# A two-layer cross-attention block on one core: the second layer attends over plain memory rows, the first loads are rearranged, and every engine follows a new sequence of steps

## The reference

```python
x = rms_norm(hidden, ln_in_w)
mixed = where(vm, x @ v_qkv, x @ l_qkv)          # two experts, chosen by token types
q, k, v = split(mixed); rotary on q, k           # 16 heads of 16
hidden += where(vm, ctx @ v_dense, ctx @ l_dense) # ctx: causal self-attention within a sequence
hidden += cross_attention(rms_norm(hidden), encoder)   # 16 heads of 8
m = rms_norm(hidden)                             # SwiGLU, inner width 688, two experts
hidden += where(vm, mlp(m, v_gate, v_up, v_down), mlp(m, l_gate, l_up, l_down))
```

```python
mem = M @ W_mem.T
mc = softmax(h @ mem.T / 16) @ mem
g = sigmoid(concat(h, mc) @ W_gate.T + b_gate)
out = rms_norm(h + g * mc) * norm_w
```

## Time and profile before

| | us |
|---|---|
| median of 3 runs | 482.73 |
| lowest and highest run | 481.61, 486.07 |
| span of the profiled execution | 474.8 |
| PE busy | 427.1 (90%) |
| DVE busy | 355.7 (75%) |
| ACT busy | 252.7 (53%) |
| POOL busy | 134.3 (28%) |

### The profile page before, as it was taken

How to read it: one execution, slowest core, us unless ns; L and a number is a source line. 1 busy time by engine, 2 the same in 40 slices (tenths; PEclk the granted TensorE clock), 3 DMA queues, 4 the chain that set the end, 5 groups by cost and what they waited for, 6 DMA issues and landing times.

```text
span 474.8 us, 10858 instructions
## 1 busy us (share of the span) xinstructions
PE 427.1 (90%) x3844; PEld 333.2 (70%) x3844; DVE 355.7 (75%) x810; ACT 252.7 (53%) x706; POOL 134.3 (28%) x246
## 2 busy tenths in 40 slices
PE   1769989899699999999999999999998999799992
PEld 1648767776468679678677777867866688487882
DVE  4888898877887898798699699699784466056575
ACT  3354458667644555556565475564462444466652
POOL 3475213232242032124114204203022100436323
PEclk9998999999989999999999999999998999999997
DMA  7813243864421112102102202111004100213111
GB/s 231 296 58 113 65 150 120 259 220 161 138 68 57 35 31 94 46 24 85 62 12 79 80 1 79 59 33 30 19 23 133 46 23 11 77 46 101 55 43 58
DMA packets 27314, 39.44 MB, mean 83 GB/s; under 512 B 3968, under 2 KB 21376, under 8 KB 27264
## 3 DMA queue, kind: packets, MB, share of 16 engines
q1 hardware_dynamic: 24128, 28.24, 18.4%
q0 software_dynamic: 3136, 10.52, 6.8%
HBM read 25.12 MB, written 13.63 MB: 82 GB/s over the span
## 4 chain that ended last, share of the span: by engine, by line
PE 66%; DVE 18%; ACT 6%; DMA 4%; issue 4%; POOL 1%; SPq 1%; POOLq 0%; ACTq 0%; DVEq 0%
PE b_ps L1653 7%; PE xyz L1540 6%; PE xyz L1499 6%; PE xyz L1526 4%; PE b_ps L1407 4%; DVE E L1144 4%; PE b_ps L1656 3%; PE b_ps L1409 3%; DVE mx L1142 3%; PE b_ps L1408 3%; PE xyz L1738 2%; PE xyz L1407 2%; PE xyz L1409 2%; PE xyz L1408 2%; PE b_ps L1667 2%
## 5 line engine op out<-in xcount | busy, mean ns | idle before, releaser
L1142 DVE TENSOR_REDUCE mx<-xyz 128x8 f32<-128x512 f32 x64 | 43.7, 683 | 5.8 <-PE xyz L1499 5.2
L1499 PE MATMUL xyz<-kT,qT 32*64 32x128 f32 (+1 forms) x768 | 44.1, 328 | 2.3 <-DVE kT L265 0.7
L1144 DVE TENSOR_TENSOR E<-xyz,mx 128x512 f32<-128x512 f32 x64 | 44.3, 691 | 2.2
L1526 PE MATMUL xyz<-cst,E 128*128 128x128 f32 x256 | 36.3, 279 | 3.6 <-ACT E L827 2.7
L259 POOL TENSOR_TENSOR qk<-E 128x256 f32<-128x256 f32 x16 | 14.2, 885 | 87.5 <-DVE E L1124 87.5
L1653 PE MATMUL b_ps<-w_gu_hi,ms_hi 128*128 (+2 forms) x90 | 37.9, 421 | 1.0 <-ACT ms_hi L851 0.6
L863 ACT ACTIVATE th<-b_ps,mrh 128x256 f32<-128x256 f32 (+1 forms) x45 | 20.2, 449 | 33.2 <-PE b_ps L1656 33.2
L1540 PEld LDWEIGHTS xyz<-vb,kT 128*64 128x64 f32 x1024 | 32.4, 138 | 6.9 <-issue 4.8
L1540 PE MATMUL xyz<-vb,kT 128*64 128x18 f32 (+1 forms) x1024 | 34.8, 219 | 2.3 <-DVE kT L1194 1.8
L1526 PEld LDWEIGHTS xyz<-cst,E 128*128 128x128 f32 x256 | 29.2, 142 | 10.3 <-ACT E L827 6.6
L1499 PEld LDWEIGHTS xyz<-kT,qT 32*64 32x64 f32 x768 | 20.7, 134 | 20.8 <-issue 9.0
(11 more groups left out here) (322 smaller groups left out, 1221.5 us busy)
## 6 DMA issues: line engine op xcount, KB each, us to landing
qkv_rows<-qrow SPq DMA_DIRECT2D x13, 384.0 KB, 2.6
...
```

The costliest lines, as they stand in the source:

```text
L1142: dve.tensor_reduce(mx[:, t, heads], s, AX.X, ALU.max).then_inc(max_ready, 1)
L1144: dve.tensor_tensor(E[t][:, b * 512:(b + 1) * 512].rearrange("p (h k) -> p h k", k=SEQ), s, mx[:, t, heads].unsqueeze(2).to_broadcast([P, ...
L1499: last = pe.matmul(xy[t][q, hp, o:o + w], qT[t][rows, c, q], kT[t][rows, (2 * c + b) * w:(2 * c + b + 1) * w], start=not masked, stop=True ...
L1526: last = pe.transpose(xy[t][:, a // 4, (a % 4) * P:(a % 4 + 1) * P], E[t][:, a * P:(a + 1) * P], ident)
```

## The change

Layer 1: `mem` exists for eight steps only. A step k transposes the plain memory of tiles 2k and 2k+1 (`mem_rows`) and makes the projected keys of tile k (`mem_keys`) in the same bank; ACT copies all with one instruction. So tiles 0 to 7 have their keys projected ahead and skip `hw`; their scores are h times keys, two products. Tiles 8 to 15 keep `hw` and the scores over plain memory. For all tiles a new step `mctx` weighs the plain memory rows, ACT copies the result, and `gate` multiplies it with `w_memT` (512 columns in one product), in place of the two products with projected memory. The wait for a free set moves from `mem` to `h3T`.

Start: the constants come in two transfers (`load_id`, `load_cst`), and all first loads stand in SP's list (W0: load_types:0 load_ln:0 load_id:0 q_in:0 q_in:1 load_cst:0, then load_w:0 to load_w:3, load_xs:2, q_in:2, load_ca:0, load_zero:0, load_w:4, load_w:5, load_xs:3, q_in:3, load_xs:1). A copy of one column is ACT's first instruction. The first products wait for each chunk of a split weight and not for both.

Order: all lists of all stages are new. In the middle stages the same step of both tiles mostly stands side by side, one `qkT` and sometimes a `cdense` cross a stage's border, and in W2 DVE and POOL begin with rope:4 and rope:5. The diff, cut to its core:

```diff
-        mpg = [late_piece(u, H, 3 * H) for u in range(NB)]
+        mcT = [late_piece(u, H, H + P) for u in range(NB)]
+        mem_rows = [late_piece(i // 2, 4 * H + i % 2 * P, 4 * H + (i % 2 + 1) * P) for i in range(N_TILES)]
+        mem_keys = [late_piece(u, 5 * H, 6 * H).rearrange("p (c k) -> p c k", c=HC) for u in range(NB)]
         mw = [late_piece(u, 3 * H, 3 * H + P) for u in range(NB)]
         hwT = mw
         mwT = [late_piece(u, 3 * H + P, 4 * H) for u in range(NB)]
-        z = [late_piece(u, 4 * H, 5 * H) for u in range(NB)]
-        w_gate2 = mpg[1].rearrange("p (c n) -> p c n", c=HC)
+        w_gate2 = late_piece(1, H, 3 * H).rearrange("p (c n) -> p c n", c=HC)
...
             ("W0", dict(
...
                 dve="""
-                    route_t:0 rank:0 wsplit:0 rank2:0 q_T:0 wsplit:1 wsplit:2 wsplit:3 q_T:1 pos:0 q_out:0 rank3:0
-                    q_out:1 q_T:2 q_out:2 table:0 rope:0 q_out:3 rope:1 qkT:0 wsplit:4 q_out:4 qkT:1 score:0 score:1
...
+                    route_t:0 pos:0 q_T:0 wsplit:0 wsplit:1 rank:0 table:0 wsplit:2 wsplit:3 q_out:0 rank2:0 q_T:1 rank3:0
+                    q_out:1 rope:0 q_T:2 q_out:2 q_out:3 rope:1 qkT:0 qkT:1 q_out:4 score:0 score:1 q_out:5 probT:0
...
                 pool="""
-                    q_sq:0 q_sq:1 x_sort:4 x_sort:5 x_sort:6 x_sort:7 rope:0 rope:1 q_sq:2 x_sort:8 x_sort:9 x_sort:10
-                    x_sort:11 x_sort:12 x_sort:13 x_sort:14 x_sort:15 q_sq:3 q_sq:4 q_sq:5 dense:0 q_sq:6 dense:1
-                    q_sq:7 rope:2 q_sq:8 rope:3""",
+                    q_sq:0 q_sq:1 x_sort:4 x_sort:5 x_sort:6 rope:0 x_sort:7 rope:1 q_sq:2 x_sort:8 x_sort:9 x_sort:10
+                    x_sort:11 x_sort:12 x_sort:13 x_sort:14 x_sort:15 q_sq:3 q_sq:4 q_sq:5 q_sq:6 dense:0 dense:1""",
...
             ("W3", dict(
...
                 dve="""
-                    qkT:6 qkT:7 score:6 miT:2 score:7 gu0:2 gu1:2 probT:6 probT:7 gu2:2 hT0:2 pv:6 pv:7 hT1:2 ctxT:6
-                    dense:6 ctxT:7 miT:3 down:2 dense:7 gu0:3 cscore:6 gu1:3 cscore:7 gu2:3 cprobT:6 hT0:3 cprobT:7
-                    hT1:3 cpv:6 rope:8 cpv:7 rope:9 cdense:6 down:3 cdense:7""",
+                    qkT:6 qkT:7 miT:2 down:1 score:6 gu0:2 score:7 gu1:2 gu2:2 probT:6 probT:7 hT0:2 hT1:2 pv:6 pv:7
+                    ctxT:6 ctxT:7 miT:3 down:2 dense:6 dense:7 gu0:3 cscore:6 cscore:7 gu1:3 gu2:3 cprobT:6 cprobT:7 hT0:3
+                    hT1:3 rope:8 cpv:6 cpv:7 rope:9 cdense:6 cdense:7""",
...
                 pe="""
-                    qkT:6 qkT:7 score_a:6 score:6 score_a:7 miT:2 score:7 gu0:2 probT:6 gu1:2 probT:7 gu2:2 hT0:2 pv:6
-                    pv:7 hT1:2 ctxT:6 ctxT:7 miT:3 dense:6 down:2 h1T:6 dense:7 cproj:6 gu0:3 cscore_a:6 h1T:7
-                    cscore:6 cproj:7 gu1:3 cscore_a:7 cscore:7 gu2:3 cprobT:6 hT0:3 cprobT:7 hT1:3 cpv:6 cpv:7 cctxT:6
-                    down:3 cctxT:7 cdense:6 cdense:7""",
+                    miT:2 qkT:7 score_a:6 score_a:7 score:6 gu0:2 score:7 gu1:2 gu2:2 probT:6 probT:7 hT0:2 hT1:2 pv:6
+                    pv:7 miT:3 ctxT:6 ctxT:7 down:2 dense:6 dense:7 h1T:6 gu0:3 h1T:7 cproj:6 cproj:7 cscore_a:6
+                    cscore_a:7 cscore:6 cscore:7 gu1:3 gu2:3 cprobT:6 cprobT:7 hT0:3 hT1:3 cpv:6 cpv:7 down:3 cctxT:6
+                    cctxT:7 qkT:8 cdense:6 cdense:7""",
             ("W7", dict(
                 sp="""
-                    m_in:10 m_in:11 m_out:10 m_out:11""",
+                    m_in:10 m_out:9 load_x:14 load_ca:14 m_in:11 m_in:12 load_cb:0 m_out:10 m_out:11""",
...
                 pool="""
-                    m_sq:10 sort:12 m_sq:11 dense:14 dense:15 sort:13""",
+                    rope:14 rope:15 sort:12 sort:13 dense:14 m_sq:11 dense:15""",
...
             ("MID", dict(
...
                 pe="""
-                    miT:12 gu0:12 gu1:12 gu2:12 hT0:12 mem:0 mem:1 hT1:12 down:12 miT:13 miT:14 gu0:13 gu1:13 gu2:13
-                    gu0:14 miT:15 hT0:13 hT1:13 gu1:14 down:13 hT0:14 gu2:14 gu0:15 gu1:15 hT1:14 down:14 miT:16
-                    gu2:15 hT0:15 gu0:16 hT1:15 gu1:16 gu2:16 down:15 hT0:16 hT1:16 mem:2 down:16 mem:3 mem:4 mem:5
-                    mem:6 mem:7""",
+                    gu0:12 gu1:12 gu2:12 hT0:12 hT1:12 mem:0 down:12 miT:13 miT:14 gu0:13 gu1:13 gu2:13 gu0:14 hT0:13
+                    hT1:13 miT:15 gu1:14 down:13 gu2:14 gu0:15 hT0:14 hT1:14 gu1:15 gu2:15 down:14 miT:16 hT0:15 hT1:15
+                    gu0:16 gu1:16 down:15 gu2:16 hT0:16 hT1:16 down:16 mem:1 mem:2 mem:3 mem:4 mem:5 mem:6 mem:7""",
             ("L1", dict(
...
                 pe="""
-                    h3T:0 hw:0 h3T:1 hw:1 h3T:2 mscore:0 h3T:3 mscore:1 hw:2 hw:3 h3T:4 attnT:0 mscore:2 mscore:3
-                    gate:0 attnT:1 hw:4 h3T:5 h3T:6 h3T:7 mscore:4 attnT:2 gate:1 mem:8 gate:2 attnT:3 hw:5 hw:6
-                    attnT:4 mscore:5 h3T:8 mem:9 mscore:6 hw:7 gate:3 gate:4 hw:8 attnT:5 h3T:9 mem:10 gate:5 h3T:10
-                    mscore:7 attnT:6 mscore:8 hw:9 mem:11 mem:12 hw:10 h3T:11 attnT:7 attnT:8 mscore:9 mscore:10
-                    gate:6 hw:11 attnT:9 mem:13 gate:7 mscore:11 h3T:12 mem:14 h3T:13 gate:8 attnT:10 h3T:14 mem:15
-                    hw:12 hw:13 h3T:15 attnT:11 mscore:12 hw:14 gate:9 mscore:13 mscore:14 hw:15 attnT:12 gate:10
-                    attnT:13 gate:11 attnT:14 mscore:15 gate:12 gate:13 attnT:15 gate:14 gate:15""",
+                    h3T:0 h3T:1 mscore:0 mscore:1 h3T:2 attnT:0 h3T:3 mscore:2 attnT:1 mctx:0 mscore:3 h3T:4 mctx:1 gate:0
+                    h3T:5 gate:1 attnT:2 attnT:3 h3T:6 h3T:7 mscore:4 mscore:5 h3T:8 mscore:6 mctx:2 mscore:7 hw:8 mctx:3
+                    gate:2 attnT:4 attnT:5 gate:3 mctx:4 mctx:5 mscore:8 h3T:9 attnT:6 attnT:7 gate:4 mctx:6 mctx:7 h3T:10
+                    gate:5 h3T:11 gate:6 h3T:12 gate:7 h3T:13 attnT:8 hw:9 h3T:14 hw:10 hw:11 hw:12 hw:13 h3T:15 mscore:9
+                    mscore:10 hw:14 mscore:11 hw:15 mctx:8 mscore:12 mscore:13 attnT:9 gate:8 attnT:10 attnT:11 mctx:9
+                    attnT:12 mscore:14 mctx:10 attnT:13 mscore:15 gate:9 attnT:14 mctx:11 attnT:15 mctx:12 mctx:13 gate:10
+                    mctx:14 mctx:15 gate:11 gate:12 gate:13 gate:14 gate:15""",
-            sp.dma_start(types_t[:, :, :].rearrange("p a i -> p (a i)"), d["types_t"]).then_inc(S["ld_cst"], 16)
-            sp.dma_start(cst[:, :], d["consts"]).then_inc(S["ld_cst"], 16)
-            sp.dma_start(ln[:, :, :].rearrange("p i c -> p (i c)"), d["ln"]).then_inc(S["ld_ln"], 16)
+            def load_types(n, t):
+                sp.dma_start(types_t[:, :, :].rearrange("p a i -> p (a i)"), d["types_t"]).then_inc(S["ld_types"], 16)
+
+            def load_id(n, t):
+                sp.dma_start(ident, d["consts"][:, C_ID:C_ID + P]).then_inc(S["ld_id"], 16)
+
+            def load_cst(n, t):
+                sp.dma_start(cst[:, C_ID + P:C_END], d["consts"][:, C_ID + P:C_END]).then_inc(S["ld_cst"], 16)
+
+            def load_ln(n, t):
+                sp.dma_start(ln[:, :, :].rearrange("p i c -> p (i c)"), d["ln"]).then_inc(S["ld_ln"], 16)
+
...
             def mem(n, t):
-                u, turn = late_set(n, t)
-                act.wait_ge(S["mem_ps"], tl(n, t))
-                act.activation(mpg[u], L[u], ACT.Copy, scale=0.5).then_inc(S["mem_ready"], 1)
+                k = index(n, t)
+                act.wait_ge(S["mem_ps"], k + 1)
+                act.activation(late_piece(k, 4 * H, 6 * H), L[k], ACT.Copy, scale=H ** -0.5).then_inc(S["mem_ready"], 1)
...
-                act.wait_ge(S["hw_ps"], tl(n, t))
+                act.wait_ge(S["hw_ps"], tl(n, t) - NB)
...
+            def mctx(n, t):
+                u, turn = late_set(n, t)
+                act.wait_ge(S["mc_ps"], tl(n, t))
+                act.activation(mcT[u], L[u][:, 0:P], ACT.Copy, scale=0.5 * H ** 0.5).then_inc(S["mc_ready"], 1)
...
+            act.wait_ge(S["blank"], 1)
+            act.activation(ss4[:, 0:1], m_sqr[:, 0:1], ACT.Copy).then_inc(S["table_in"], 1)
+            act.wait_ge(S["table_in"], 1)
...
-                dve.wait_ge(S["ld_cst"], 32)
+                dve.wait_ge(S["ld_id"], 16)
                 dve.tensor_copy(ident_h[:, :], ident)
                 dve.tensor_tensor(ident_q[:, :, :], ident[:, 0:SEQ].unsqueeze(1).to_broadcast([P, 2, SEQ]),
                                   ident[:, SEQ:P].unsqueeze(1).to_broadcast([P, 2, SEQ]), ALU.add)
+                dve.wait_ge(S["ld_cst"], 16)
...
-                if r < 2:
-                    pe.wait_ge(S["wsplit_lo"], HC * (r + 1))
                 for c in range(HC):
+                    if r < 2:
+                        pe.wait_ge(S["wsplit_lo"], HC * r + c + 1)
...
             def mem(n, t):
-                i, (u, turn) = index(n, t), late_set(n, t)
-                if i == 0:
+                k = index(n, t)
+                if k == 0:
                     pe.wait_ge(S["ld_cb"], 16 * 4)
                     pe.wait_ge(S["catt_ready"], N_TILES)
-                if turn:
```

(45 more changed lines are left out.)

270 lines of the change are left out of this document (133 added, 137 removed).

## The result

The changed kernel took 478.06 us (476.57 to 479.4, 9 runs), the kernel before 482.73 (480.49 to 486.07, 9 runs): a ratio of 0.9895 [0.987, 0.992], 4.7 us less, where 13.2 less was forecast. The time lies in my range and the sign is right; the gain is a third of the forecast one. The profiled execution took 476.7 us for a span of 474.5.

The account below looks back on a forecast made before the run. PE was taken as the bound, DVE close behind in the middle and a mixture before W2. Terms -5.2, -1.0, -3.5, -2.0, -1.5 and 0 sum to -13.2 us, from 482.7 to 469.5, range 459 to 480.

Parts of the forecast that it names:

- The last layer, -5.2: Layer 1: less PE work from dropped `mem` and `hw` steps, saving 5.2 us net, bounds -6.5 and -2.
- MID, -1.0 and -3.5: MID: fewer `mem` steps before `down:16` save 1.0 us; expert slot 12's wait and low clock at its start go, 3.5.
- Start -2.0: Kernel start: earlier table load, first product and `x_sort` issues save 2.0 us, bounds 0 and -4.5.
- W0 to W2 -1.5: New order at 126 to 132 us: PE waits less for DVE's splits and ropes, saving 1.5 us, bounds +2 and -4.
- W2 to W6, order. The work is the same ... I book 0.: Middle stages: reordered steps move stalls without net gain, 0 us booked, bounds -1.2 and +1.2 a stage over six stages.
- The sign that I had named: Middle stages: the prediction is wrong if the steady period leaves 37.3 to 39.3 us, or L1 saves less than 3.
- So 7.9 us lie around the span: Whole kernel before: median run 482.73 us against a 474.8 us span, with 7.9 us taken to lie around the span.
- B: Rival, whole kernel: only L1's counted saving of 5.2 us arrives, MID and start gains are given back; 477.5 us, chance 0.14.
- D: Rival, no change: L1's saving is lost to new waits and stages cost 0.8 us each; 479.5, up to 483, chance 0.12.

Follow-up runs that it names:

- z1: The changed kernel, unaltered, on a chip where the kernel before takes 477.19 us: 463.81 us, ratio 0.9721.
- v2: The kernel before, unaltered, run again with a profile on a chip where it takes 482.63 us: 483.87 us, ratio 1.0018.
- v4: The changed kernel, unaltered, on a chip where the kernel before takes 482.63 us: 477.46 us, ratio 0.9908.
- x1: The kernel before with only layer 1 new (lists and code), old start and old lists through MID: 472.13 us against 476.98, ratio 0.9896.
- v1: The changed kernel with old lists in W3 to W6, miT:10 and m_sq:10 moved at the join to W7: 474.46 us against the kernel before's 482.63, ratio 0.9838.
- y2: The changed kernel with old lists in W3 to W6, run again on a chip where the kernel before takes 477.02 us: 465.97 us, ratio 0.9769.

## Why the forecast came out as it did

Both kinds of chip have a pair of profiles. The start of the second h2 sum of a group, of the last y and the end of the last `fin`, in us (the first column is the trace of before that I worked from):

| | before | z1 | difference | v2 (before) | v4 (after) | difference |
|---|---|---|---|---|---|---|
| group 0 | 78.4 | 77.3 | -1.1 | 81.5 | 83.7 | +2.2 |
| group 2 | 171.2 | 165.7 | -5.5 | 177.3 | 173.0 | -4.3 |
| group 6 | 324.5 | 318.8 | -5.7 | 330.7 | 330.4 | -0.3 |
| group 7 | 362.8 | 357.0 | -5.9 | 369.0 | 369.4 | +0.4 |
| last y | 405.3 | 395.5 | -9.8 | 410.5 | 408.1 | -2.4 |
| last fin | 470.3 | 456.8 | -13.5 | 477.5 | 470.7 | -6.8 |

**The last layer, -5.2: right in its mechanism.** From the first gather's issue to the end it is 4.5 us shorter on both kinds (62.07 to 57.56 us, and 64.14 to 59.68); alone it gave 4.4 and 4.9 in the times. From the first `h3T` to PE's end it took 50.4 us in `z1` and 51.7 in the first profile, where I had said 49 to 51 and no `gm_ready` wait: there is none. The hand-over from the last y to the first gather I had booked at nothing. It takes 2.9 us in the three traces of the kernel before and 3.0 to 4.0 in the four of the changed kernel, so it costs up to 1.1 us. Why isn't shown.

**MID, -1.0 and -3.5: right in kind, 0.6 too much in sum.** It took 38.6 us for 42.5, -3.9 on kind 1, and 38.7 for 41.5 on kind 2. In `z1` the first product of slot 12 runs at 356.40 with no wait, and the clock is 1.00 over the stage. With the new layer 1 alone (`x1`) MID took 41.1, so the `mem` steps are 1.4 of it (for 1.0) and the start 2.6 (for 3.5).

**Start -2.0 and W0 to W2 -1.5: low on kind 1**: -5.5 by group 2, of which W1 gives 2.8 (50.65 us for 53.46). The low-clock stretch at 126 us is gone in `z1`; I had counted half its wait and nothing for the clock. That this is the whole difference is argued from the traces, not tested. The table load is as forecast: 1.28 us at 0.73, and the next ACT instruction starts 0.02 us behind it, so the drain of the Trainium skill's page ("ScalarE: Activation LUTs", section "What ACT_TABLE_LOAD costs") isn't seen here either.

**The step that failed: "W2 to W6, order. The work is the same ... I book 0."** The work is the same, and on kind 1 it does cost nothing: group 2 to group 6 took 153.1 us for 153.4. On kind 2 it cost 4.0 us (157.4 for 153.4), and with W7 4.7, since the new lists put the scores of a tile beside `sort` and `get` on GpSimd; with the old lists in `v1` three of the four stages are back at 38.3 to 38.5. I had walked the stage with waits between engines free, as the trace of before has them. My bound of 1.2 us a stage holds for the mean of these stages (1.0) and not for single ones. The pair of traces on kind 2 ends 6.8 us apart where I had said 13.2, and this term is 4.7 of the 6.4 that lack. The rest is MID (-2.8 for -4.5) and the stretch from the last y to the end (-4.4 for -5.2); the first three stages gave a little more than I had said (-4.3 for -3.5). **The start** failed for the same reason, by the sign: -1.1 on kind 1, +2.2 on kind 2, where PE, DVE and ACT pause between 32 and 43 us while the `x_sort` issues follow each other, and the clock behind is 0.74 [the window at 40 us above]. Both kernels pay there, the changed one more (6.3 us for 3.1 by group 0).

**The sign that I had named.** "The prediction is wrong if the steady period leaves 37.3 to 39.3." It left it on both kinds: W4 and W5 took 40.1 and 40.9 us in the first profile, W5 and W6 40.0 and 36.9 in `z1`. On kind 1 nothing is lost by it, since work moved across the border of the two stages (W6 has 382 of PE's instructions). W4 and W5 in `z1`, PE's count behind its busy time:

```profile
203.90:241.90 38.00, 36.21 (x401) 28.99 (x400) 32.27 (x71) 23.90 (x67) 9.06 (x17) 1.00 0.20 61
241.90:282.00 40.10, 37.64 (x420) 29.82 (x419) 34.25 (x77) 20.05 (x57) 11.18 (x21) 1.00 0.19 54
```

So of the 2.7 us that W5 has over 38.3 in the first profile, some 1.7 are this shift. The sum of several stages is the better sign.

**Luck on kind 1.** 13.4 us for 13.2 looks exact, and the terms are not. In the traces the part up to group 2 gave 2.0 us more than I had booked, MID 0.6 less and the stretch from the last y to the end 1.5 less (-3.7 for -5.2); they happen to cancel.

**The base.** "So 7.9 us lie around the span" was wrong: 1.8 to 2.2 do. The profile was an execution of some 477 us and the median one of 482.7; six microseconds of the kernel before stood in no row I had. I saw the gap and took it for a constant. The first trace of the kernel before has the marks of kind 1: 3,197 records of landings, and one wait of the listed sort, of 0.36 us. The times of the comparison and the changed kernel's profile are of kind 2. So my rows came from a chip without the pauses, and the forecast was set against one that has them. The gap between span and time was the one sign of it beforehand. None of the rivals named the cause. B comes nearest in time (477.5): the last layer's saving arrives, as it says, but MID keeps most of its gain, and most of what is lost is lost in W3 to W7. D (479.5) has the stages at 0.8 us each, which is near, but its other half, the last layer's saving lost, is false.

**A version for both kinds.** `v1`/`y2` (the change with the old lists in W3 to W6) is below the kernel before on both kinds: 0.9838 and 0.9769. The changed kernel is better on kind 1 by 2 us (0.9721, on another chip), worse on kind 2 by 3 us (0.9908).
